# One block for latent attention, output mix and two window layers: where the mix and the first window tiles are issued

## The reference

```
x = attn_x                                             # (4, 1024, 128)
x = x + layernorm(attention(layernorm(x)))             # 16 heads of 8, causal, low-rank q/k/v, then W_o
y = layernorm(x)
for l in 0, 1:                                         # two window layers
    h = shift_token(y)                                 # second half of the channels one token later
    q, k, v = split(h @ wqkv[l])                       # 8 heads of 64
    q, k = l2norm(q) * qs, l2norm(k) * ks ; rotary with xpos scales
    y = y + local_attention(q, k, v) @ wo[l]           # windows of 64, each sees itself and the one before
    h = layernorm(shift_token(y)) * lg + lb
    h = h @ w1 + b1 ; y = y + (a * gelu(g)) @ w2 + b2
out = x + layernorm(y)
```

## Time and profile before

| | us |
|---|---|
| median of 3 runs | 1399.64 (1396.19 to 1404.19) |
| profiled execution, its own time | 1401.46 |
| span of its instructions | 1399.4 |
| PE busy | 1251.4 |
| DVE busy | 1107.0 |
| ACT busy | 930.4 |
| POOL busy | 744.3 |

### The profile page before, as it was taken

How to read it: one execution, slowest core, us unless ns; L and a number is a source line. 1 busy time by engine, 2 the same in 40 slices (tenths; PEclk the granted TensorE clock), 3 DMA queues, 4 the chain that set the end, 5 groups by cost and what they waited for, 6 DMA issues and landing times. The chain is left out here.

```text
span 1399.4 us, 30218 instructions
## 1 busy us (share of the span) xinstructions
PE 1251.4 (89%) x10501; PEld 713.6 (51%) x10501; DVE 1107.0 (79%) x2921; ACT 930.4 (66%) x2469; POOL 744.3 (53%) x772
## 2 busy tenths in 40 slices
PE   4689999999999999638999999989989999997895
PEld 2323333333333433515666666656556666665663
DVE  5788888888888881457999999766589999998675
ACT  4526776777767776466888888732478888886334
POOL 1112122221222212339999999923399999998244
PEclk9859999999999998669999999999999999999998
DMA  4432111111111100301111111100012111111001
GB/s 107 124 101 71 50 55 44 39 37 53 53 44 39 38 6 3 104 8 31 40 44 29 30 31 32 32 1 1 16 24 52 32 32 32 33 32 24 1 16 45
DMA packets 35053, 55.44 MB, mean 40 GB/s; under 512 B 6978, under 2 KB 22732, under 8 KB 32588
## 3 DMA queue, kind: packets, MB, share of 16 engines
q1 hardware_dynamic: 34328, 53.37, 14.5%
q10 hardware_dynamic: 576, 0.15, 0.0%
HBM read 26.77 MB, written 8.39 MB: 25 GB/s over the span
## 5 line engine op out<-in xcount | busy, mean ns | idle before, releaser
L533 ACT ACTIVATE a_prob<-a_psE 128x512 f32<-128x512 f32 (+1 forms) x608 | 306.4, 583 | 147.9 <-PE a_psE L457 146.8
L443 PE MATMUL a_psM<-a_ks,a_qs 72*128 72x512 bf16 (+3 forms) x768 | 248.3, 343 | 10.9 <-DVE a_nm L619 3.7
L569 POOL TENSOR_SCALAR_AFFINE_SELECT a_prob<-a_prob 128x512 f32<-128x512 f32 x128 | 80.9, 634 | 327.9 <-ACT a_prob L533 326.5
L617 DVE CUSTOM_DVE_ANT_0 a_psM<-a_psM,mask_q 128x384 f32<-128x384 f32 (+3 forms) x512 | 242.2, 507 | 15.5 <-PE a_psM L443 15.0
L457 PE MATMUL a_psE<-a_qs,a_ks 84*128 84x512 bf16 (+3 forms) x768 | 240.7, 335 | 12.5 <-ACT a_prob L533 7.3
L1302 POOL TENSOR_TENSOR w_rn<-w_ssm,mhalf 128x16 f32<-128x16 f32 x64 | 214.5, 3352 | 48.0 <-DVE w_ssm L1401 32.6
L619 DVE TENSOR_REDUCE a_nm<-a_psM 128x1 f32<-128x512 f32 x256 | 175.6, 686 | 45.8 <-PE a_psM L443 45.8
L1193 ACT ACTIVATE w_prob<-w_psS,w_bias 128x128 f32<-128x128 f32 x512 | 179.8, 376 | 22.4 <-DVE w_bias L1427 22.4
L1292 POOL TENSOR_TENSOR w_t<-w_raw,w_sin 128x256 f32<-128x256 f32 x256 | 178.5, 729 | 0.0
L1297 POOL TENSOR_TENSOR w_rot<-w_t 128x1024 f32<-128x1024 f32 x64 | 150.9, 2358 | 8.8 <-issue 0.4
L457 PEld LDWEIGHTS a_psE<-a_qs,a_ks 84*128 84x128 bf16 x768 | 74.9, 99 | 151.8 <-ACT a_prob L533 70.4
(11 more groups left out here) (150 smaller groups left out, 2400.0 us busy)
## 6 DMA issues: line engine op xcount, KB each, us to landing
w_vb_<-w_v_ SPq DMA_DIRECT2D x128, 128.0 KB, 2.3
a_qs<-q_parts SPq DMA_DIRECT2D x16, 576.0 KB
a_ks<-k_parts SPq DMA_DIRECT2D x16, 576.0 KB
q_parts<-p_parts SPq DMA_DIRECT2D x24, 128.0 KB
k_parts<-p_parts SPq DMA_DIRECT2D x24, 128.0 KB
out_x<-x_sb SPq DMA_DIRECT2D x8, 256.0 KB, 2.3
a_qs<-a_nmT SPq DMA_DIRECT2D x32, 48.0 KB
w_wqkv<-in_wqkv SPq DMA_DIRECT2D x2, 768.0 KB, 7.6
```

Source lines behind the costliest of these rows:

```text
L443: pe.matmul(out, qs[0:ROWS, g, j, i * P:(i + 1) * P], ks[0:ROWS, g, j, 512 * kc:512 * kc + n], start=True, stop=True).then_inc(m_ready, 1)
L533: act.activation(prob[G % NPROB][:, j - share + 1:j + 1, 0:w], psE[:, r % NRING, 0:share * w].rearrange("p (j n) -> p j n", j=share), ACT. ...
L617: dve.tensor_tensor_reduce(scores, scores, sb["mask_q"][:, 512 - n:512], -1.0, -3.0 * NEG, ALU.add, ALU.min, low).then_inc(m_read, 1)
```

## The change

The blocks `attend`, `mix` and `layers` become one block, `attend_and_layers`; `project` stays a block. Tiles of different stages of the program now lie on the same bytes of one arena (`shelf`), each laid where a tile that is no longer read has been; `psM`'s banks become `w_psQK`, `w_psT0_` and `w_psV`, and `psE`'s become `w_psS` and `w_psT1_`. The statements inside the steps of attention and layers are the same but for names.

- **Mix.** Each half of a batch is turned three groups behind its last `outputs` and projected two groups later, through slots of the ring `psE`; ACT copies the projection to SBUF (`attn`), and the moments are taken from there. In terms of G within a stage (stages counted from 0): for batch b, halves 0 and 1 are turned in group 11 of stage 4b+3 and group 7 of stage 4b+4, and projected in groups 1 and 9 of stage 4b+4. The moments follow in groups 2 and 10, the power in 11, the norm by ACT in groups 1 and 2 of stage 4b+5, sum and second moments by DVE in groups 3 and 4, the second norm by ACT in groups 7 and 8. The power is taken for eight columns at once. Batches 0 to 2 run so; of batch 3 half 0 is turned in the last group and projected behind it, half 1 goes through `psO` in slot 1 of the layers, and the rest of its mix goes in slots 1 to 8.
- **First window tiles.** `turn_x` of tiles 0 to 3, q and k of tiles 0 and 1, v of tiles 0 and 1, with their copies, squares, sums, cosines and carries, are issued in the last 14 groups; q and k of tile 2 follow the last `values`. POOL does `norms(0)`, `rotate(0)` in the ninth group from the end and tile 1 in the last. Slots -2 to 0 are gone, and PE's loop begins at slot 1.
- **Tables.** The cosines and sines are loaded into `w_cos` and `w_sin` themselves and scaled there; for layer 1 SP loads them anew when layer 0's last tile has used them.
- **Loads.** W_o, wqkv, scales and carry are loaded once the parts are out, before stage 0's first wait; the tables at the end of stage 13, the mask and wo at the end of stage 14.

```diff
+def turn_group(b, h):
+    return o_turn_group(NG * b + NG - 1, h) + 3
+def project_group(b, h):
+    return turn_group(b, h) + 2
...
         @block.sync
+            load_weights(sp, io, sb)            # w_o, carry, per layer wqkv and two scales
             for e in range(NSTAGE):
                 if e + 1 < NSTAGE:
                     send_maxima(e + 1, 0)
+                if e == NSTAGE - 2:
+                    sp.wait_ge(av_done, e * NGR)
+                    load_tables()
...
+            sp.wait_ge(av_done, (NSTAGE - 1) * NGR)
+            load_late_weights(sp, io, sb)       # mask_w, wo of both layers
...
         @block.tensor
+            def turn_o(b, h):
+                pe.wait_ge(m_read, o_slot(NG * b + NG - 1, h) + 1)
...
+                    r = E_SLOT["t", b, h]
+                    ge(pe, e_read, r - NRING + 1)
+                    out = psE[:, r % NRING, :]
+                for t in range(4):
+                    mm = pe.transpose(out[:, t * P:(t + 1) * P], sb["o_tok"][:, TB * b + 4 * h + t, :], sb["ident"])
...
+            def window_head(G):
+                if G == LAST_G - 12:
+                    pe.wait_ge(m_read, M_TAIL)
+                    turn_x(0)
+                if G == LAST_G - 10:
+                    turn_x(1)
+                    pe.wait_ge(w_in, W_LOADS)
+                    project_qk(0)
+                if G == LAST_G - 8:
+                    project_v(0)
+                if G == LAST_G - 6:
+                    pe.wait_ge(m_read, M_TAIL + 1)
+                    turn_x(2)
+                    project_qk(1)
+                if G == LAST_G - 4:
+                    project_v(1)
+                if G == LAST_G - 2:
+                    pe.wait_ge(m_read, M_TAIL + 2)
+                    turn_x(3)
...
             for G in GROUPS[-AV_LAG:]:
                 values(G)
+            project_o(B - 1, 0)
+            project_qk(2)
             turn_outputs(NSTAGE - 1, 1)
-            for s in range(-2 if layer == 0 else 0, NT - 1):
+            for s in range(1 if layer == 0 else 0, NT - 1):
...
         @block.scalar
+            def window_head(G):
+                if G == LAST_G - 11:
+                    act.wait_ge(zeroed, 2)
+                    copy_hT(0)
+                if G == LAST_G - 9:
+                    copy_hT(1)
+                if G == LAST_G - 8:
+                    copy_raw(0)
+                if G == LAST_G - 7:
+                    squares(0)
+                    copy_v(0)
+                if G == LAST_G - 5:
+                    copy_hT(2)
+                if G == LAST_G - 4:
+                    copy_raw(1)
+                if G == LAST_G - 3:
+                    copy_v(1)
+                if G == LAST_G - 2:
+                    squares(1)
+                if G == LAST_G - 1:
+                    copy_hT(3)
...
         @block.gpsimd
+                for b in range(B - 1):
+                    for w in range(2):
+                        if project_group(b, 1) + 2 + 6 * w == G:
+                            powers_m(w, b)
+                if G in (LAST_G - 8, LAST_G):
+                    T = (G - LAST_G + 8) // 8
+                    pool.wait_ge(tables, 6)
+                    norms(T)
+                    rotate(T)
...
         @block.vector
+            def mix_step(G):
+                for b in range(B - 1):
+                    for h in range(2):
+                        if project_group(b, h) + 1 == G:
+                            moments_a(b, h)
+                        if project_group(b, 1) + 6 + h == G:
+                            add_a(b, h)
+                        if project_group(b, 1) + 6 + h == G:
+                            moments_x(b, h)
+                    for w in range(2):
+                        if project_group(b, 1) + 3 + 6 * w == G:
+                            shift_m(w, b)
```

More of the change, by code:

```diff
@@ L13 @@
+import math
 from contextlib import ExitStack
@@ L830, in layers, with early @@
-def layers(nc, io, sb):
-    with ExitStack() as ctx:
-        def tile(name, shape, dt=F32):
+        def early(name, shape, dt=F32):
             return ctx.enter_context(nc.sbuf_tensor(name, shape, dt))
@@ L837, in sem @@
             return ctx.enter_context(nc.semaphore(name))
-        wqkv, wo = sb["wqkv"], sb["wo"]
+        arena = sb["arena"]
+        NPROB, NRING, MRING = 5, 3, 4
+        qs, ks, v_flat = sb["qs"], sb["ks"], sb["v_flat"]
+        tile = shelf(nc, arena + PROB_AT)
+        prob = [tile(f"a_prob{r}", [P, HG, 512]) for r in range(NPROB)]
+        oT = tile("a_oT", [P, 2, 512])
+        nmT = tile("a_nmT", [NM, 2, S], BF16)
+        nm = early("a_nm", [P, 2, 2, TB, HG])
+        nmr = early("a_nmr", [P, 2, 4 * HG])
@@ L924, in _, with max_unit @@
         def _(pe):
+            def max_unit(u):
+                s, (i, j, kc) = u // NMU, MAX_UNITS[u % NMU]
+                g, r = s % NG, max_slot(u)
+                if u % NMU == 0:
+                    pe.wait_ge(stack_in[g], 32 * (s // NG + 1))
+                n = min(512, (i + 1) * P - 512 * kc)
+                out = psM[:, m_bank(r), 0:n]
+                ge(pe, m_read, r - MRING + 1)
+                pe.matmul(out, qs[0:ROWS, g, j, i * P:(i + 1) * P], ks[0:ROWS, g, j, 512 * kc:512 * kc + n],
+                          start=True, stop=True).then_inc(m_ready, 1)
@@ new lines, in project_o @@
+            def project_o(b, h):
+                if (b, h) == (B - 1, 1):
+                    pe.wait_ge(m_oT_copied, 1)
+                    out = psO
+                else:
+                    r = E_SLOT["p", b, h]
+                    pe.wait_ge(e_read, E_SLOT["t", b, h] + 1)
+                    ge(pe, e_read, r - NRING + 1)
+                    out = psE[:, r % NRING, :]
+                for t in range(4):
+                    mm = pe.matmul(out[:, t * P:(t + 1) * P], ocT[:, t, :], sb["w_o"], start=True, stop=True)
+                mm.then_inc(m_oT_done if (b, h) == (B - 1, 1) else e_ready, 1)
@@ L1252, in _ @@
                 final = layer + 1 == DEPTH
-                for s in range(-2 if layer == 0 else 0, NT + 1):
+                for s in range(1 if layer == 0 else 0, NT + 1):
                     window_slot(layer, s)
@@ new lines, in _ @@
+            for G in range(-1, NSTAGE * NGR):
+                for u in range(max_until(G - 1) if G >= 0 else 0, max_until(G)):
+                    maximum(u)
+                    if u % NMU == NMU - 1:
+                        merge(u // NMU)
+                for e in range(max(0, G // NGR - 1), G // NGR + 1):
+                    for qc in range(2):
+                        if G >= 0 and o_turn_group(e, qc) == G:
+                            outputs(e, qc)
+                mix_step(G)
+                window_head(G)
@@ L1542, in _ @@
                 final = layer + 1 == DEPTH
-                for s in range(-2 if layer == 0 else 0, NT):
+                for s in range(1 if layer == 0 else 0, NT):
                     window_slot(layer, s)
```

1029 lines of the change are left out of this document (547 added, 482 removed).

## The result

| | before | changed |
|---|---|---|
| median of the runs, us | 1399.05 (1396.19 to 1404.19, 7 runs) | 1388.66 (1380.43 to 1389.53, 7 runs) |
| span of the profiled execution, us | 1399.4 | 1386.9 |
| mean granted clock of the span | 0.950 | 0.957 |

The changed kernel takes 0.9913 of the time of before (95% interval 0.9889 to 0.9937). That is 10.4 us less, where 40 less had been forecast and the range ended at 1382. The direction was right. The size was wrong, and the time is outside the range that was given.

The account below looks back on a forecast made before the run. PE and DVE were taken to bound the attention in turn, with 70.2 us of latency between two nearly full stages. 1401.46 - 69.9 + 21 + 3 + 6 = 1361.6, so a median of 1360 us; range 1336 to 1382.

Parts of the forecast that it names:

- What goes: Between the last outputs and the first turn_qk: only semaphores remain there, so 69.9 us go.
- Mix of batches 0 to 2: In the attention stages: added PE, DVE and ACT work costs 7 us a batch, 21 us for three.
- Edits at nothing: Early loads, table loads, new SBUF places and merged blocks: no cost, or a few us once if bytes delay the maxima.
- The head in the last 14 groups: In the attention's tail: the layers' first steps lengthen it from 34.27 to 37.3 us, +3; bounds -4 and +8.
- The first slots: In layer 0's first slots: batch 3's mix costs +6 us, between +1.5 for POOL alone and +10.6 in series.
- After the slots: From POOL's power of tile 12 to the end: no change, 0; layer 1 of unchanged length.
- D: In the six stages with mix: its stalls take PE's clock down, 1423 us, slower than before; chance 0.03.
- B: In mix, tail and first slots: bursts run in series, 40 + 8 + 10.6 = 58.6, 1388 us; chance 0.07.
- C: In the tail: head not hidden, PE waits for hT and raw; +18 over the forecast, 1378 us; chance 0.08.

Follow-up runs that it names:

- e8: On e1, sums and second moments of a batch's two halves in groups 3 and 6 instead of 3 and 4, followers two groups later; 1366.73 us, one run.
- e2: Changed kernel with only the four small scale loads moved behind stage 2's maxima, the other early loads left early; 1394.13 us in one run.
- e1: Changed kernel with W_o, wqkv, scales and carry loaded after stage 2's maxima instead of before stage 0's; 1371.99 us, ratio 0.9801.
- e5: On e1, PE's six head steps in the tail moved one group later, into groups without values products; 1364.90 us, ratio 0.9746.
- e9: The edits of e1, e5, e7 and e8 together in one kernel, no other edit; 1358.38 us, ratio 0.9703.
- e10: On e9, PE's head steps put between the scores of a group, q and k of a tile apart; 1357.89 us, ratio 0.9701.
- e12: On e9, each score product of the last 14 groups issued twice into the same place; 1360.36 us, ratio 0.9715.
- e3: Changed kernel with the head steps of the tail put behind the last outputs, tables still scaled in the tail; 1391.6 us in one run.
- e4: Changed kernel without the mix of batch 3, whose layer input is a copy of x; 1376.89 us in one run.
- e7: On e1, batch 3's two powers on POOL after tiles 3 and 7 instead of 2 and 6, followers one slot later; 1366.96 us, ratio 0.975.
- e6: On e1, the values products put before the head step in the same odd groups of the tail; 1370.74 us, ratio 0.9793.

## Why the prediction was wrong, step by step

**What goes (-69.9): right.** The gap shrank by 69.0. The first `turn_qk` follows the last `outputs` in 1.2 us, and POOL's power of tile 2 starts 5.8 after that (617.2), near the 6.9 of before. But it came at 611.37 and not near 589: all that the prediction missed up to there stands in the attention and its tail.

**Mix of batches 0 to 2 (+21): right, 18.4 measured.** It is 6.1 a batch in place of 7. Stages without it kept 28.9. The prediction had PE's own work (2.9 of 8.2) and DVE's two bursts (2.4) as the largest parts; e8, which puts the bursts three groups apart instead of one, gives 1.4 back. The place was right, the size somewhat less. The prediction had two stages a batch get longer. There are three: the one after, 29.9, holds only one us more than it should, which goes away with e8.

**Edits at nothing (0): the step that failed most, 14.2 measured.** The sentence was "the issue hides, and if the bytes delay them, a few us once". The issue did hide, as e2 shows: 7.5 us less of it changed PE's wait by 0.8. The bytes didn't. The prediction counted that the maxima "are not ready until later" and didn't ask when they arrive: already before, that was at about 127, behind 2.3 MB of stacks and just ahead of their use at 128.42. With 1.5 MB more ahead of them it was about 136. An estimate from the bytes gets there (1.5 MB at the 160 to 200 GB/s of most slices from 106 to 115 is 8 to 10 us), but partly by luck, as the queue moved only 76 GB/s while the maxima were awaited. The wait was 7.0. The prediction also priced a wait at its own length, when the clock came down to 0.50 during it and 6.4 us more were lost before it rose. e1, which moves one line, gives back 15.7 us by the ratios.

**The head in the last 14 groups (+3): failed, +12.8, and above its bound of +8.** The bound for "wrong" was a tail over 42. Three things are in it, and the runs part them:

- *The order.* From e1 to e5 the tail goes from 48.3 to 40.9, and with the clock as near as it comes, from e8's 43.0 (0.96) to e5's 40.9 (0.92), it is 2.1 or somewhat more. The prediction gave each engine's sum of work and asked if it fitted. It did fit, but it asked nothing about one piece: 1.02 + 1.71 us of PE between two scores at the full clock and 1.91 + 3.63 at the lower one, against three banks that hold under 2 us of work for ACT.
- *The clock.* The same instructions ran 43.0 us at 0.96 and 51.2 at 0.77. The prediction had this as its bound, 39.4 instead of 34.3 for PE, and took the middle. What it didn't see is that the order may decide also this. In the six kernels with the order of changed the clock was 0.76 to 0.96, and in the six with another order it was 0.92 to 1.00. PE waits for ACT 6.0 us in changed's tail and 4.3 in e9's, which fits. But the link is argued and not shown: e8 has the bad order and 0.96.
- *PE's idle, put at nothing.* In the good orders 39.3 to 41.4 remain, 5 to 7 over 34.3, with the clock at 0.92 to 1.00. The prediction's 34.3 and 39.4 are busy times of PE, held against a length of 34.27. But PE was busy only 29.65 of it, so both bounds left out 4.6 us of idle. In e10 PE is busy 34.40 of 39.28, and the idle is still there: 4.9. An estimate from the two rows, with (1 - clock) times the length as the part lost to the clock, makes PE's work at the full clock 29.65 - 5.1 = 24.5 before and 34.40 - 1.6 = 32.8 in e10. That is 8.3 more work (9.7 in the prediction), 3.5 less lost to the clock and 0.3 more idle, together the 5 us by which e10's tail is longer. In changed the idle is 7.0. It isn't a fixed price, since e12's 56 products leave only 1.4 of it; but no order tried here filled it with the head's steps.

So of the 70.2 us of latency removed, some 18 were the head of the layers as e3 runs it, and of the 16.5 that could be saved of it, changed saved 3.2 in this pair of profiles. From the last merge to the first `turn_qk` e5 takes 42.1 and e10 40.5 us, so they save 9.4 and 11.0.

**The first slots (+6): mechanism right, size off, 9.7 measured.** e4 shows that all of it is batch 3's mix. The prediction charged POOL 2.0 for each of the two powers with its addition. One cost 1.85. The other, behind a wait of 1.64 for DVE's moments, cost 3.82. POOL, forecast as over 95% busy, was busy 77.25 of 88.63. Up to tile 12 it waited 8.9 us for DVE's sums of squares (`w_ssm`), where it had waited 2.3 before. So the +6, half way between POOL alone and everything in series, was too near the first. e7, which asks for them one slot later, got the stretch down to 101.6, which is the +6 of the forecast.

**After the slots (0): right, 1.4 measured.** Nearly all of it lies between POOL's power of tile 31, the last of layer 0, and that of tile 35, a stretch with the MLP part of layer 0 and the head of layer 1: 132.8 before, 134.0 in changed. It varies between the kernels from 130.0 (e3, e4) to 135.0 (e1) with the same instructions, which no experiment explains. It is the larger part of why e3's 5.5 us at tile 12 were 2.9 at the end.

**The rivals.** D needed a clock of 0.75 in the stages with mix; it was 1.00 there. It had the right mechanism in the wrong place: a wait brought PE's clock down in the one stage that was thought to be untouched. B foretold 1388 and was right in number by chance: its 40 + 8 + 10.6 were mix, tail and slots, and measured were 18.4, 12.8 and 9.7, with 14.2 of loads that it hadn't. C comes nearest in substance for the tail, without its stated cause: in changed's tail all of PE's waits that the trace shows are for ACT's exponentials (6.0 us), none for hT or raw, and ACT stood waiting for scores (15.0). The range of 46 us would have held any one of the four misses, of 14.2, 9.8 and 3.7 us too much and 2.6 too little, but not even the first two of them together.

## What to carry to other kernels

Before a bulk load is called free, put its bytes in front of the next small transfer of the same queue, read from the trace when that one arrives now and how long before its use, and price the wait with the slower clock behind it: here 7.0 us of waiting cost 13.4, and moving one line gave it back. When work is put into a stream between two engines, compare its longest unbroken piece with what the ring between them holds, since the sum of busy times doesn't show it: six steps placed one group later gave 7 us, about half of them by way of the clock. And when busy times are added to see whether work fits, add the idle that the stretch already has: here 4.6 us of it stayed. Latency that is removed at a joint comes back where its work lands if the new neighbours are also a chain, so ask of each moved step what it makes late.

## What the runs showed of the hardware

- *The same tail at two clocks.* Kernels whose tails are alike instruction by instruction had it at 0.76 to 0.96, 51.2 to 43.0 us. It isn't only between kernels: seven runs of changed lie between 1380.43 and 1389.53, four of e7 between 1362.91 and 1374.76, and those of e9 within 2.3 us. With the shorter pieces in the tail (e5, e9 to e12) all spreads are under 3.5 us; in e1, e6 and e7, with the longer ones, they are 5.8 to 11.9.
- *POOL after a wait.* An addition over 8 columns took 0.20 us in a stream and 1.09 after a wait of 1.64; the power behind it took 1.65 and 2.73. That is one pair in one trace, about 1 us more for each operation, and no run shows what it comes from.
- *SP's issues.* In changed SP took 0.33 to 0.43 us over some loads, and 4.26 over each of two 32 KB loads of scales issued behind some 3 MB (four stacks of 576 KB, and the first 768 KB of `wqkv`). It cost next to nothing here, as e2 shows, since SP does nothing but issue transfers. The Trainium skill, "DMA: Bandwidth & Descriptors", section "🔬 Queues, rings and completion order", says that SP owns one ring on each of the 16 engines and that each engine takes descriptors in the order of its ring. The wait of 6.19 us in e2, for a transfer whose issue had begun 22 us before, fits that.
- *A queue that isn't full can still be late.* While PE waited for the maxima the DMA engines were busy 0.22 of the time, as much as three or four of the sixteen, and moved 76 GB/s; before, 0.22 and 84.
